# A layer of graph attention and routed experts on one core: each token goes through its two experts' pages only

## What is computed

```python
xn = _layernorm(x, axis=-1)                       # x: 6250 nodes x 256, src and dst: 100000 edges
x = x + gnn(xn, ..., src, dst) + mix(xn, ...)     # graph attention, and linear attention of 8 heads
x = x + moe(_layernorm(x, axis=-1))

def moe(tokens, ...):                             # 8 experts, each 256 -> 256 -> 256
    probs = softmax(tokens @ router_w.T)
    rw, re = top_k(probs, 2); rw = rw / rw.sum(-1)
    combine = zeros((N, 8)).at[arange(N)[:, None], re].set(rw)
    out = tokens
    for e in range(8):
        h = gelu(tokens @ w1[e] + b1[e])
        out = out + combine[:, e:e + 1] * (h @ w2[e] + b2[e])
```

## Time and profile before

| | |
|---|---|
| runs, median of 3 (lowest, highest) | 2007.62 us (2007.61, 2009.14) |
| profiled execution: span, first to last instruction | 2207.5 us, 40303 instructions |
| its mean granted clock of TensorE | 0.895 |
| busy: PE, DVE, POOL, ACT | 1718.1, 1669.8, 994.8, 976.2 us |
| moved by DMA | 182.21 MB, mean 83 GB/s |

### The profile page before, as it was taken

How to read it: one execution, slowest core, us unless ns; L and a number is a source line. 1 busy time by engine, 2 the same in 40 slices (tenths; PEclk the granted TensorE clock), 3 DMA queues, 4 the chain that set the end, 5 groups by cost and what they waited for, 6 DMA issues and landing times.

```text
span 2207.5 us, 40303 instructions
## 1 busy us (share of the span) xinstructions
PE 1718.1 (78%) x13588; PEld 1259.6 (57%) x13588; DVE 1669.8 (76%) x4220; ACT 976.2 (44%) x2300; POOL 994.8 (45%) x988
## 2 busy tenths in 40 slices
PE   3778785574785688888757888887888888889998
PEld 2557573463674466666535555555555555566666
DVE  5998998663566677776767887888888888886665
...
GB/s 174 16 59 52 51 66 32 42 84 115 145 165 130 118 120 119 102 94 90 90 90 87 86 90 83 94 83 94 82 95 92 86 92 83 89 56 11 11 20 13
DMA packets 121460, 182.21 MB, mean 83 GB/s; under 512 B 21490, under 2 KB 91902, under 8 KB 121214
## 3 DMA queue, kind: packets, MB, share of 16 engines
...
...
## 4 chain that ended last, share of the span: by engine, by line
DVE 42%; PE 23%; issue 16%; another core or an unknown queue 10%; ACT 4%; DVEq 2%; POOL 1%; DMA 0%; SPq 0%; ACTq 0%; POOLq 0%
PE bank L1255 6%; PE bank L1271 5%; DVE mloc L1615 4%; DVE big L1518 4%; DVE scr L1637 3%; DVE big L1523 3%; DVE work L1809 3%; DVE big L1520 2%; DVE big L1525 2%; DVE big L1796 2%; DVE scr L1483 2%; DVE work L1593 2%; DVE work L1610 2%; PE bank L947 1%
## 5 line engine op out<-in xcount | busy, mean ns | idle before, releaser
L664 POOL DMA_INDIRECT work<-table,tiles x904 | 921.0, 1019 | 546.6 <-PE bank L1142 277.8
L1271 PE MATMUL bank<-big 128*128 128x256 f16 x2352 | 327.7, 278 | 34.8 <-issue 34.5
L1255 PE MATMUL bank<-scr,big 128*128 128x512 f16 (+1 forms) x1248 | 282.3, 377 | 0.3 <-ACT big L871 0.3
L1140 PE MATMUL bank<-work,scr 128*128 128x257 f16 x904 | 269.9, 299 | 13.0 <-issue 10.5
L1271 PEld LDWEIGHTS bank<-big 128*128 128x128 f16 x2352 | 232.3, 99 | 78.3 <-issue 46.0
L1141 PE MATMUL bank<-work,scr 128*128 128x256 f16 x904 | 270.8, 300 | 5.9 <-issue 5.6
L1142 PE MATMUL bank<-work,scr 128*128 128x257 f16 x904 | 268.9, 297 | 5.9 <-issue 5.9
L1637 DVE SCALAR_TENSOR_TENSOR scr<-scr,gg,bank 128x257 f32<-128x257 f32 x452 | 216.7, 479 | 29.7 <-remote 16.6
L999 PE MATMUL bank<-big 128*128 128x208 f16 x1568 | 176.9, 269 | 67.7 <-DVE big L1525 60.9
L799 ACT ACTIVATE work<-bank 128x1024 f16<-128x1024 f16 x113 | 115.5, 1022 | 242.7 <-DVE mloc L1615 144.0
L999 PEld LDWEIGHTS bank<-big 128*128 128x128 f16 x1568 | 150.7, 102 | 94.6 <-issue 88.9
...
## 6 DMA issues: line engine op xcount, KB each, us to landing
work<-table,tiles POOLq DMA_INDIRECT x904
...
```

Source lines behind the costliest of these rows:

```text
L664: pool.indirect_dma_start(G[:, r, j, :], None, table, bass.IndirectOffsetOnAxis(ap=col[:, t:t + 1], axis=0)).then_inc(rows_in[r // GS], 16)
L1140: pe.matmul(of[:, 0:D + 1], hi, Gh[:, r, j, 0:D + 1], start=(j == 0), stop=False)
L1255: mm = pe.matmul(bank[5 + f][:, 0:n * P], w1p[pw][:, e, h, f * P:(f + 1) * P], x2p[b % 2][px][:, h, 0:n * P], start=(h + m == 0), stop=(h ...
L1271: mm = pe.matmul(of, hTp[ph][:, k % 2, f, (j + c) * P:(j + c + 1) * P], w2p[pw][:, e, f, :], start=False, stop=(f == 1 and m == 2))
```

## The change

Experts' work is done on pages. After routing, a count over all tiles of a round gives each token two slots (its two experts' next free places); a page is 256 slots of one expert. POOL scatters each tile's normed rows, as high and low half-precision parts (1 KB), to its two slots in memory. Units of two pages are loaded, turned on TensorE, put through the page's expert, whose weights are loaded from memory as one packed set, and written back. Each tile's two results are fetched with two indirect DMAs and added with their weights. There are four rounds, of 16, 16, 12 and 5 tiles, with 23, 23, 19 and 12 pages. Slots are zeroed during the first part. By the code, placing stands in steps 60, 82, 110 and 123, sends from 61, 83, 111 and 124, the 40 units' turns in steps 71 to 149 (every second), up one step later and down two, outputs in steps 115 to 159. The rest of the diff, left out here, renames or merges semaphores, and gives buffers other places; four hand-written chains of increment and wait become the helper `link`, which does the same.

```diff
+    ROUNDS = ((0, 4), (4, 8), (8, 11), (11, NBAT))
+    NR = len(ROUNDS)
+    FIRST_TILE = [NB * b for b, _ in ROUNDS] + [W]
+    of_round = [FIRST_TILE[r + 1] - FIRST_TILE[r] for r in range(NR)]
+    PG = 2 * P
+    pages = [(2 * P * n + X * (PG - 1)) // PG for n in of_round]
+    slots = [nc.dram_tensor(f"slots{r}", [pages[r] * PG, 2 * D], F16).ap() for r in range(NR)]
+    ys = [nc.dram_tensor(f"ys{r}", [pages[r] * PG, D], F32).ap() for r in range(NR)]
+    chosen = nc.dram_tensor("chosen", [X * P, WROW // 2], F32).ap()
...
-            at_ += X
-        UP_AT = {F_AT[b] + e: (b, e) for b in range(NBAT) for e in range(X)}
-        DOWN_AT = {t + 1: k for t, k in UP_AT.items()}
-        ADD_AT = {t + 2: k for t, k in UP_AT.items()}
-        S_END = max(ADD_AT) + 1
+            at_ += 4
         FIRST = {F_AT[b]: b for b in range(NBAT)}
...
+        PLACE_AT = {F_AT[z - 1] + 1: r for r, (_, z) in enumerate(ROUNDS)}
+        round_of = [r for r in range(NR) for _ in range(of_round[r])]
+        SEND_AT, UNITS, T_AT, STORED = {}, [], {}, []
+        t_ = 0
+        for r in range(NR):
+            first = F_AT[ROUNDS[r][1] - 1] + 2
+            for i in range(of_round[r]):
+                SEND_AT.setdefault(first + i // 3, []).append(FIRST_TILE[r] + i)
+            t_ = max(t_, first + (of_round[r] - 1) // 3 + 5)
+            for u in range(0, pages[r], 2):
+                T_AT[t_] = len(UNITS)
+                UNITS.append((r, u, min(2, pages[r] - u)))
+                t_ += 2
+            STORED.append((len(UNITS), t_ + 1))
+        UP_AT = {t + 1: k for t, k in T_AT.items()}
+        DOWN_AT = {t + 2: k for t, k in T_AT.items()}
+        OUT_AT, t_ = {}, NS + 2
+        for r in range(NR):
+            t_ = max(t_, STORED[r][1] + 1)
+            for i in range(of_round[r]):
+                OUT_AT.setdefault(t_, []).append(FIRST_TILE[r] + i)
+                t_ += 1 if t_ < max(DOWN_AT) else i % 2
+            t_ += 1
+        S_END = max(OUT_AT) + 1
+        POOL_SEND = {}
+        for s, v in SEND_AT.items():
+            POOL_SEND.setdefault(s + 3 if s + 3 < NS else max(s, NS), []).extend(v)
+        POOL_OUT = {s - 1: v for s, v in OUT_AT.items()}
...
+                if ZERO * (i + 2) < len(blanks):
+                    for o in blanks[ZERO * (i + 2):ZERO * (i + 3)]:
+                        sp.dma_start(o, tiles[:, 0:D].bitcast(F16)).then_inc(zeroed, 16)
...
+            def expert_sets(k):
+                r, u, n = UNITS[k]
+                sp.wait_ge(p_done, r + 1)
+                if k > 1:
+                    sp.wait_ge(u_y, HALF0[k - 1])
+                for h in range(n):
+                    i = 2 * (k % 2) + h
+                    sp.reg_load(eid, eidt[0:1, PAGE0[r] + u + h:PAGE0[r] + u + h + 1])
+                    e = sp.snap(eid, min_val=0, max_val=X - 1)
+                    sp.dma_start(sets[i], chosen[ds(e * P, P), :]).then_inc(set_in[i], 16)
+            def slot_rows(k):
+                r, u, n = UNITS[k]
+                for i in range(XROWS):
+                    sp.wait_ge(sent[i], 32 * len(range(i, FIRST_TILE[r + 1], XROWS)))
+                if k > 1:
+                    sp.wait_ge(u_t, k - 1)
+                sp.dma_start(xr[k % 2][:, 0:2 * n, :], slots[r][u * PG:(u + n) * PG, :].rearrange("(c p) f -> p c f", p=P)
+                             ).then_inc(xr_in[k % 2], 16)
+            def y_rows(k):
+                r, u, n = UNITS[k]
+                for h in range(n):
+                    sp.wait_ge(u_yc, HALF0[k] + h + 1)
+                    sp.dma_start(ys[r][(u + h) * PG:(u + h + 1) * PG, :].rearrange("(c p) d -> p c d", p=P), ysb[h]
+                                 ).then_inc(y_out[h], 16)
...
+                if s == B2_AT + 2:
+                    sp.wait_ge(b_parts, 1)
+                    to = chosen.rearrange("(e p) c -> p e c", p=P)
+                    for n in range(4):
+                        sp.dma_start(to[:, :, n * D:(n + 1) * D], big[:, n * WE // 2:(n + 1) * WE // 2].rearrange(
+                            "p (e f) -> p e f", e=X)).then_inc(chosen_out, 16)
+                    sp.dma_start(to[:, :, 4 * D:4 * D + D // 2], big[:, 2 * WE:2 * WE + X * D // 2].rearrange(
+                        "p (e d) -> p e d", e=X)).then_inc(chosen_out, 16)
+                    sp.dma_start(to[:, :, 4 * D + D // 2:WROW // 2], b1c[:, :].rearrange("p (e h) -> p e h", e=X)
+                                 ).then_inc(chosen_out, 16)
+                    sp.wait_ge(chosen_out, 16 * 6)
+                if s + 2 in T_AT:
+                    expert_sets(T_AT[s + 2])
+                if s + 1 in T_AT:
+                    slot_rows(T_AT[s + 1])
+                if s in DOWN_AT:
+                    y_rows(DOWN_AT[s])
+                for j in OUT_AT.get(s, ()):
+                    out_rows(j)
...
+            def send(j):
+                r, i = round_of[j], j % XROWS
+                pool.wait_ge(p_done, r + 1)
+                pool.wait_ge(d_lo, j + 1)
+                for k in range(2):
+                    pool.indirect_dma_start(slots[r], bass.IndirectOffsetOnAxis(ap=posi[:, j, k:k + 1], axis=0),
+                                            xrows[i], None).then_inc(sent[i], 16)
+            def fetch(j):
+                r, i = round_of[j], j % YG
+                if j >= YG:
+                    pool.wait_ge(o_sum, j + 1 - YG)
+                for h in range(2):
+                    pool.wait_ge(y_out[h], 16 * sum(n > h for _, _, n in UNITS[:STORED[r][0]]))
+                for k in range(2):
+                    pool.indirect_dma_start(yg[i][:, k, :], None, ys[r],
+                                            bass.IndirectOffsetOnAxis(ap=posi[:, j, k:k + 1], axis=0)
+                                            ).then_inc(yg_in[i], 16)
+            for s in range(max(NS, max(POOL_SEND) + 1, max(POOL_OUT) + 1)):
+                for j in POOL_SEND.get(s, ()):
+                    send(j)
+                for j in POOL_OUT.get(s, ()):
+                    fetch(j)
...
+            def row_hi(j):
+                act.wait_ge(p_done, round_of[j] + 1)
+                if j >= XROWS:
+                    act.wait_ge(sent[j % XROWS], 32 * (j // XROWS))
+                if j > 1:
+                    act.wait_ge(d_lo, j - 1)
+                act.reg_load(wid, wids[0:1, j:j + 1])
+                x_w = xs[:, ds(act.snap(wid, min_val=0, max_val=W - 1), 1), :].rearrange("p a c -> p (a c)")
+                act.activation(x2f[j % 2], x_w, ACT.Identity, bias=rsp[:, 2, j:j + 1], scale=rsp[:, 0, j:j + 1]
+                               ).then_inc(d_x2, 1)
+                act.wait_ge(d_x2, j + 1)
+                act.copy(xrows[j % XROWS][:, 0:D], x2f[j % 2]).then_inc(d_hi, 1)
+            def slots_turned(k):
+                n = UNITS[k][2]
+                for h in range(n):
+                    act.wait_ge(u_t, HALF0[k] + h + 1)
+                    if k and h == 0:
+                        act.wait_ge(u_up, k)
+                    act.copy(xT[:, :, :, h * PG:(h + 1) * PG],
+                             bank[5 + h][:, :].bitcast(F16).rearrange("p (k h n) -> p k h n", k=2, h=2)).then_inc(u_x, 1)
+            def hidden(k):
+                n = UNITS[k][2]
+                act.wait_ge(u_up, k + 1)
                 if k:
+                    act.wait_ge(u_lo, k)
+                for h in range(n):
+                    for f in range(2):
+                        ins = act.activation(hT[:, f, h * PG:(h + 1) * PG], bank[5 + f][:, h * PG:(h + 1) * PG], ACT.Gelu,
+                                             bias=b1s[2 * (k % 2) + h][:, f:f + 1])
+                ins.then_inc(u_g, 1)
+                act.wait_ge(u_g, k + 1)
                 if k > 1:
+                    act.wait_ge(u_y, HALF0[k - 1])
+                act.copy(hTp[0][:, k % 2, :, 0:n * PG], hT[:, :, 0:n * PG]).then_inc(u_hi, 1)
...
+            def choices_counted(r):
+                b = ROUNDS[r][1]
+                j, n = FIRST_TILE[r], of_round[r]
+                pe.wait_ge(m_one, b)
+                if halves_done[0]:
+                    pe.wait_ge(u_yc, halves_done[0])
+                of = oneh[:, j:j + n, :, :].rearrange("p w k e -> p e (w k)")
+                pe.matmul(bank[7][:, 0:2 * X * n], ladder[:, :], of, start=True, stop=True)
+                pe.matmul(bank[1][:, 0:2 * X * n], onesq[:, :], of, start=True, stop=True).then_inc(p_ps, 1)
+            def slots_turned(k):
+                n = UNITS[k][2]
+                pe.wait_ge(xr_in[k % 2], 16 * (k // 2 + 1))
                 if k:
+                    pe.wait_ge(u_g, k)
+                for h in range(n):
+                    for c in range(2):
+                        for part_ in range(2):
+                            for f in range(2):
+                                at = (2 * part_ + f) * PG + c * P
+                                mm = pe.transpose(bank[5 + h][:, :].bitcast(F16)[:, at:at + P],
```

(48 more changed lines are left out.)

462 lines of the change are left out of this document (247 added, 215 removed).

## The result

The changed kernel takes **2424.84 us** in the median of 4 runs (2417.87 to 2427.17), the kernel before 2008.07 (2007.61 to 2009.14, 4 runs): ratio **1.2068**, 95% interval 1.2047 to 1.2089. The prediction had slower as the likelier side, but its 2030 us and its range to 2100 are far too low. The profiled execution of the changed kernel spans 2422.9 us, the same as its runs.

The account below looks back on a forecast made before the run. VectorE was taken to bound the aggregation steps, TensorE the tail before the change. Terms of -59 (steps, placing, sends), +79 (tail) and +5 (before step 47) gave +25 on a 2207.5 us span, scaled to 2030 us; range 1950 to 2100.

Parts of the forecast that it names:

- Sends: Two indirect DMAs per tile on POOL, ahead of the gathers: 28 us charged for both bursts, ends 0 and 82.
- POOL may be up to two steps ahead: In the bursts of sends, POOL's lead over the steps was to cover 22 us, regained at under 1 us a step.
- steps wider by 3 to 6 us: Sign of the prediction: steps 61 to 66 and 83 to 88, with the sends, widen by 3 to 6 us each.
- The tail: Steps 111 on: 20 us of steps, 19.5 units at 12.4 us, 38 us output; 300 us, 79 more than before.
- Ordinary steps: Steps 47 to 110: less VectorE work brings a step from 12.80 to 11.2 us, 717 us in all.
- placing: Steps 60, 82 and 110: chained VectorE instructions cost 4.9 us each time, 15 us for three, none hidden; ends 6 and 25.
- VectorE sets the step: Aggregation beside experts, steps 47 to 110: VectorE, busy 697.6 of 831 us, is the bound, TensorE close, POOL ready early.
- rival C: Steps 47 to 110: POOL is the bound, 576 indirect DMAs in series, 800 us with waits; 2067 us in all; chance 9%.
- Before step 47: First part: zeroing writes hidden in SP's waits, packed sets written in step 31; 5 us for both, ends 0 and 25.
- The scale: Whole kernel: run time taken as 0.9095 of the profiled span, turning 2232.5 us into 2030 us.
- B: Rival, the clock: tail units take 14.5 us with TensorE's clock low, 341 us of units; 2090 us in all; chance 14%.
- D: Rival: too many pages or rounds waiting for their last send, so units crowd behind; 2110 us or more; chance 4%.

## Why the prediction was wrong

**Sends: this step failed, by some 180 us.** It charged 28 us for both bursts, upper end 82, since "POOL may be up to two steps ahead", 22 us that a burst could use up. They cost 209 us (107 and 102, from the run without sends), of which the wait alone makes 147 and the scatters 62. POOL's place ahead was no cover but the trap: when POOL comes to a send in its own order its row does not exist yet, and POOL cannot stand there and be ahead as well. The change adds a wait on VectorE to POOL's queue, and the prediction priced what stands behind it (the sends' own time) without asking when the thing waited for is made: at the end of step s, when the gathers behind are wanted 1 step later. The upper end of 82 us took the sends' work as the most that could be lost, and a wait has no such bound: one turn of the ring is 28 us or more where an ordinary step is 12.3, and there are twelve. The signs said so too: steps wider by 3 to 6 us were forecast in the bursts, and in the first one they are wider by 19.

**The tail: mechanism right, size off.** In the first profile the steps up to the first turn take 20.6 us (20 predicted), the units to the end of the last down 333.1 (2049.7 to 2382.8 us; 242 predicted), the outputs behind it 40.1 (38): 393.8 instead of 300. So the one term that failed is the unit, put at 12.4 us; 18 distances of turns have a mean of 17.5, the last ten 16.5. The pieces of the quoted unit: slots landed 10.8 us after the down's end (8.4 predicted), turns 1.9 (1.0) and down 3.0 (3.05), 15.7. The load takes 4.9 to 8.2 us from its issue to landing, 7.2 in the median; 351 GB/s was the rate of the kernel's first loads, and here the average is 166, with fetches, sums and outputs between. Of the turns, 16 transposes take 1.89 us in this unit and 1.05 in the quoted one of the run with slots first; the tail's granted clock is 0.70 and not 1.00 as before. The first nine units also met the sends of 17 tiles and the routing, which the prediction left out of the tail; without sends the tail is 16 us shorter. The Trainium skill, DMA: Bandwidth & Descriptors, section Queues, rings and completion order, says that each DMA engine consumes descriptors in ring order. The run with slots first agrees, 16.6 to 12.5 us, but it also issues the load before SP's wait for the down, and no run parts the two.

**Ordinary steps.** 11.2 us from 12.80 was predicted, 102 us in all, less 15 for placing. Outside the bursts the gain here is 12 us in 16 steps, 11 in 14 and 5 in 15 (91 to 106), 0.6 us a step where 1.6 was summed; the bursts without their sends took 1 and 17 us more than before (the second holds a placing and its routing). Together 10 us of gain instead of 87. VectorE's work did fall, as it was counted; in the second of the three stretches, before and after here (the third number is its busy time):

```profile
1452.90:1637.80 184.90, 152.71 (x1301) 105.34 (x1300) 151.69 (x406) 114.09 (x221) 113.61 (x113) 0.93 0.33 87
```
```profile
1548.30:1722.20 173.90, 118.91 (x1092) 91.65 (x1092) 120.14 (x343) 83.70 (x191) 107.04 (x109) 0.78 0.48 136
```

32 us less work for 11 us of time; in the third stretch 33 for 5, and only in the first 15 for 12, where four batches are routed in the steps in which before there were two. The step that failed is "VectorE sets the step": it did not go on doing so. In the changed kernel's first profile, which has no pauses, POOL has no slack left. All of 1032 to 2029 us, then 1383.2 to 1531.5 and 1740.9 to 1905.9 us, both outside the bursts:

```profile
L817 POOL DMA_INDIRECT work<-table,tiles x512 | 512.6, 1001 | 195.9 <-issue 143.2 <-PE bank L1338 52.6
...
L817 POOL DMA_INDIRECT work<-table,tiles x113 | 114.5, 1014 | 34.4 <-issue 32.0 <-PE bank L1338 2.4
...
L817 POOL DMA_INDIRECT work<-table,tiles x125 | 128.3, 1026 | 38.1 <-issue 34.1 <-PE bank L1338 4.0
```

The gathers and the 0.28 us behind each are 10.2 us for eight, and in the two stretches they fill 146.5 of 148.3 and 162.4 of 165 us; POOL waits for a ring place 2.4 and 4.0 us. These steps take 10.6 and 11.0 us, and what leaves VectorE beyond that gives nothing: rival C's bound, in a size that the prediction had as its lower end. From 1032 to 1210 us it is still VectorE, busy for 152.6 of 178. On the higher level POOL waits for ring places again (34.7 us in the second stretch), and pauses are longer than before (264 us on VectorE over the span, 214 before); what sets the step there stays open. A gather takes 1.001 us in the mean, 1.035 before. By the Trainium skill, SBUF — State Buffer, section Who interferes with whom, a tensor_tensor with both inputs in SBUF contends with GpSimd's reads, so that fewer of them would make it faster. The rows agree by that 0.03; no run has it as its only change.

**Hot row.** Not in the prediction at all: exponentials 106 to 112 take 94 us here, 94 to 110 in the kernels with this padding, 71 in the kernel before, whose padding did the same (a DMA share of 0.83 at 70 GB/s from 1939 to 2010 us) with no load of slots behind it. Spread, they take 73 to 80.

**Before step 47.** Right: 5 us predicted, -1 measured, in a mark that lies from 1161 to 1169 us in all the changed kernels here. The zeroing was hidden.

**The scale.** 0.9095 from span to time was called an assumption and was wrong in kind: there are two levels of the same kernel, and the durations came from the higher. It did not decide the miss, since both kernels shift: +403 us on one level, +417 on the other, where +25 was predicted.

The miss of 378 us, by terms, on the higher level:

| term | predicted | measured |
|---|---|---|
| before step 47 | +5 | -1 |
| ordinary steps and placing | -87 | -10 |
| sends | +28 | +209 |
| exponentials 106 to 112, hot row | 0 | +23 |
| tail and output | +79 | +182 |
| sum | +25 | +403 |

Measured terms are differences of marks; the second and third are parted by the run without sends. Of the +23, spreading the padding takes away 17.

Of the rivals, B (the tail at 14.5) had the nearest unit, and C the nearest mechanism for the steps. Only D's "2110 or more" holds the time, and by its number alone: its units were to crowd behind late sends, and here it is the aggregation that stands. None had the ring of waits.
